# Seven of every sixteen attention heads transposed by VectorE through memory, and the first network's exponentials taken ahead of its transposes

## The reference

```
# first network, layer l
scores = leaky(si[:, :, None] + sj[:, None, :] + attn_b[l]);  scores = where(mask, scores, -inf)
agg = softmax(scores) @ x
h = layernorm(x + agg, g1[l], beta1[l])
x = layernorm(h + gelu(h @ W1[l] + b1[l]) @ W2[l] + b2[l], g2[l], beta2[l])
# between and after
x = layernorm(x + first_network(x, adj))
# second network, per head
att = softmax(where(A > 0, leaky(a_src[:, None] + a_dst[None, :] + b_att), -1e30))
out = relu(att @ xh);   result = layernorm(x + concat(out))
```

## Time and profile before

| | us |
|---|---|
| median of 3 runs (2388.36 to 2389.09) | 2388.61 |
| the profiled execution | 2386.59 |
| its span | 2384.8 |
| PE busy | 2285.7 (96%) |
| ACT busy | 1775.3 (74%) |
| DVE busy | 1715.9 (72%) |

### The profile page before, as it was taken

The page is one execution under the profiler, slowest core; times in us unless marked ns, Lnnn a source line. Parts: engine busy times, 40 slices in busy tenths (PEclk is TensorE's granted clock), DMA queues, the critical chain, the costliest instruction groups (busy, mean ns, idle before and its releaser), DMA issues.

```text
span 2384.8 us, 33626 instructions
## 1 busy us (share of the span) xinstructions
PE 2285.7 (96%) x11169; PEld 1629.3 (68%) x11169; DVE 1715.9 (72%) x5676; ACT 1775.3 (74%) x3415; POOL 168.0 (7%) x200
## 2 busy tenths in 40 slices
PE   3999999999999999999999999999999999999866
PEld 2667667767776776777677777767776776777543
DVE  5455886588767877678766787668867687767587
ACT  2444478877888778887787878887788877888786
POOL 0000100000000000000000000000100000000000
PEclk9999999999999999999999999999999999999977
DMA  6011021022111132011320121210211111200011
GB/s 214 10 36 36 33 96 61 20 67 89 44 55 49 34 105 63 22 50 37 97 72 23 67 85 27 76 50 32 93 42 54 54 36 63 67 19 23 31 44 33
DMA packets 85783, 131.56 MB, mean 55 GB/s; under 512 B 4424, under 2 KB 53868, under 8 KB 85612
## 3 DMA queue, kind: packets, MB, share of 16 engines
q1 hardware_dynamic: 85612, 129.41, 16.7%
HBM read 120.74 MB, written 8.65 MB: 54 GB/s over the span
## 4 chain that ended last, share of the span: by engine, by line
PE 86%; DVE 6%; ACT 6%; issue 1%; DMA 0%; POOL 0%; SPq 0%; POOLq 0%; DVEq 0%; ACTq 0%
PE ffn L1116 25%; PE av L1041 13%; PE ffn L1105 12%; PE av L1105 12%; PE pT L1024 12%; PE av L1057 5%; ACT prob L459 2%; PE av L1092 2%; PE av L1140 1%; PE trow L1140 1%; DVE prob L703 1%; ACT prob L453 1%; PE trow L1003 1%; DVE prob L694 1%; ACT l1x L493 1%
## 5 line engine op out<-in xcount | busy, mean ns | idle before, releaser
L1116 PE MATMUL ffn<-w_sb,G 128*128 128x256 f32 x3072 | 752.5, 381 | 0.9 <-ACT G L477 0.9
L1116 PEld LDWEIGHTS ffn<-w_sb,G 128*128 128x128 f32 x3072 | 553.5, 191 | 77.9 <-issue 14.2
L1024 PEld LDWEIGHTS pT<-ident,prob 128*128 128x128 f32 x2816 | 356.2, 145 | 207.1 <-issue 121.5
L703 DVE CUSTOM_DVE_ANT_0 prob<-trow,mask 128x512 f32<-128x512 f32 x704 | 458.3, 686 | 38.8 <-PE av L1065 16.9
L1024 PE MATMUL pT<-ident,prob 128*128 128x128 f32 x2816 | 440.1, 282 | 45.9 <-DVE prob L748 16.1
L459 ACT ACTIVATE prob<-prob,nm 128x512 f32<-128x512 f32 x512 | 362.8, 711 | 0.0
L453 ACT ACTIVATE prob<-prob,s 128x512 f32<-128x512 f32 x512 | 349.2, 714 | 9.1 <-DVE nm L710 7.7
L1105 PE MATMUL ffn<-hT,w_sb 128*128 128x512 f32 x768 | 354.9, 595 | 1.1 <-ACT hT L472 1.1
L1105 PE MATMUL av<-hT,w_sb 128*128 128x512 f32 x768 | 353.3, 592 | 0.0
L468 ACT COPY prob<-pT 128x512 f32<-128x512 f32 x452 | 260.7, 581 | 101.8 <-PE pT L1024 100.3
L409 POOL TENSOR_TENSOR rstd<-veps,mhalf 128x4 f32<-128x4 f32 x127 | 152.6, 1202 | 2175.6 <-DVE veps L638 2175.6
(11 more groups left out here) (119 smaller groups left out, 2468.2 us busy)
## 6 DMA issues: line engine op xcount, KB each, us to landing
w_sb<-in_L_gnn_W SPq DMA_DIRECT2D x48, 1024.0 KB, 8.4
trow<-rows_dram SPq DMA_DIRECT2D x128, 256.0 KB, 3.2
adj_sb<-in_adj SPq DMA_DIRECT2D x16, 1024.0 KB, 5.5
xin<-in_x SPq DMA_DIRECT2D x16, 512.0 KB, 6.3
x0r<-in_x SPq DMA_DIRECT2D x16, 512.0 KB, 4.5
out<-o SPq DMA_DIRECT2D x15, 512.0 KB, 3.0
aw_row<-in_L_gnn_attn_w SPq DMA_DIRECT2D x1, 768.0 KB
g_row<-in_L_gnn_g SPq DMA_DIRECT2D x2, 384.0 KB
```

The costliest lines, as they stand in the source:

```text
L703: return v.tensor_tensor_reduce(out=out_[:, t, :], in0=targets, in1=mask[:, t, :], scale=1.0, scalar=LEAST, op0=ALU.add, op1=ALU.max, accu ...
L1024: last = te.transpose(pT[bank][:, j * P:(j + 1) * P], src[:, t, j * P:(j + 1) * P], ident[:])
L1116: last = te.matmul(ffn[part][:, at:at + D], G[:, f, t * P:(t + 1) * P], w2_sb[:, g // 2 % STAGES, f, :], start=f == 0, stop=f == FT - 1)
```

## The change

- `BY_BLOCKS` names seven of the 16 heads of a pair: 1, 2, 4, 5, 8, 10 and 13. For heads of the first six pairs of graphs (`q < LAST_HEADS - 2 * HEADS`, so 42 heads in all) TensorE's 4 turns and ScalarE's 4 copies fall away. VectorE transposes the 32x32 blocks of the whole head in one instruction into a new buffer `blocks` (`turn_blocks`), SP stores it with four DMAs into `blocks_dram`, waits for them, and loads it back into the head's place in the ring with a fifth (`move`). `attend_heads` waits for that load and reads such a head with another pattern (`sources`). In slots 2 and 4 (`AHEAD`) the second head is turned by VectorE before the attention; the others after it (`turned_behind`), and in slot 1 one of the two at the end of the unit.
- The first network's exponentials are taken by ScalarE before the transposes (`exponential0`), in place of VectorE's subtraction; what comes out of PSUM is only copied.
- Pieces 4 and 5 move ahead of the attention, pieces 6 and 7 take their place within it, and after the attention stand pieces 8 to 15.
- `times_gain` keeps the multiplication; the addition of the bias (`plus_bias`) moves to just before `fed_forward` part 0.
- `keep_masks(0)` moves from slot 4 to slot 2, `make_masks(0)` from slot 4 to slot 3.
- `trow1` holds two rows instead of three (`ROWS`), and `y_att` now lies in `prob0`, so VectorE waits for the normalised state before `scores`.

```diff
+BY_BLOCKS = (1, 2, 4, 5, 8, 10, 13)
+AHEAD = (2, 4)
+def moved(q):
+    return q < LAST_HEADS - 2 * HEADS and q % (2 * HEADS) in BY_BLOCKS
...
+            def move(q):
+                n = moves(q) - 1
+                i = n % BANKS
+                sp.wait_ge(s_block, n + 1)
+                if n >= BANKS:
+                    sp.wait_ge(s_moved, 16 * (n - BANKS + 1))
+                for a in range(BLOCKS):
+                    sp.dma_start(blocks_dram[i, :, :, a, :].rearrange("b j n -> j b n"),
+                                 blocks[a * BLOCK:(a + 1) * BLOCK, :, :]).then_inc(s_left, 16)
+                sp.wait_ge(s_left, 16 * BLOCKS * (n + 1))
+                sp.dma_start(ring(q)[:], blocks_dram[i].rearrange("b j a n -> (b j) a n")).then_inc(s_moved, 16)
...
+            def exponential0(u, t):
+                act.wait_ge(s_score0, T * u + t + 1)
+                nc.scalar.activation(prob0[:, t, :], prob0[:, t, :], ACT.Exp, bias=nm0[:, t:t + 1], scale=1.0).then_inc(s_arg, 1)
...
-                nc.scalar.activation(prob0[:, t, :], pT[t % BANKS][:], ACT.Exp).then_inc(s_prob, 1)
+                nc.scalar.copy(prob0[:, t, :], pT[t % BANKS][:]).then_inc(s_prob, 1)
...
+            def turn_blocks(q):
+                n = moves(q) - 1
+                dve.wait_ge(s_exp, T * (q + 1))
+                if n:
+                    dve.wait_ge(s_left, 16 * BLOCKS * n)
+                v.transpose(blocks[:].rearrange("p b (x i) -> p x b i", i=BLOCK),
+                            ring(q)[:].rearrange("p t (j b i) -> p (t j) b i", b=BLOCKS, i=BLOCK)).then_inc(s_block, 1)
...
                 if att:
                     if ends is not None:
                         first_network_ends(ends)
+                    for q in turned_ahead(g):
+                        turn_blocks(q)
                     attention(s2, l2, *new[1:2])
+                for q in turned_behind(g)[:1]:
+                    turn_blocks(q)
                 if done is not None:
                     graph_out()
+                plus_bias(s, l)
                 if att:
                     fed_forward(s, 0)
...
                 for q in new[2:]:
                     head_made(q)
                 if four is not None:
                     heads_out(four)
+                for q in turned_behind(g)[1:]:
+                    turn_blocks(q)
...
-                for t in range(T):
-                    piece(t)
+                for n in range(T + DT if att else T):
+                    piece(n)
                 if att:
-                    attention(s2, l2, g + 1, lambda i: piece(4 + i))
+                    attention(s2, l2, g + 1, lambda i: piece(6 + i))
...
                     for q in heads[1:2]:
-                        turn(q, t)
+                        if not moved(q):
+                            turn(q, t)
```

More of the change, by code:

```diff
@@ L29 @@
 RING = 8
-ROWS = 3
+ROWS = 2
+BLOCK = 32
+BLOCKS = P // BLOCK
 STAGES = 2
@@ L79, in turned, with moves, turned_ahead, turned_behind @@
     return made(g - 1) if g else []
+def moved(q):
+    return q < LAST_HEADS - 2 * HEADS and q % (2 * HEADS) in BY_BLOCKS
+def moves(q):
+    return sum(map(moved, range(q + 1)))
+def turned_ahead(g):
+    return [q for q in turned(g)[1:2] if moved(q) and g % SLOTS in AHEAD]
+def turned_behind(g):
+    return [q for q in turned(g)[1:] if moved(q) and q not in turned_ahead(g)]
 def side_by_side(heads):
@@ L367, in _ @@
                     load_x(2 * p + 3)
+                for q in new[1:2]:
+                    load_rows(q + 1)
+                for q in turned_behind(g)[:1]:
+                    move(q)
+                if ended(g) is not None:
+                    store_out(ended(g))
                 if k == SLOTS - 2 and not last:
@@ L519, in _ @@
             for t in range(T):
+                exponential0(0, t)
+            for t in range(T):
                 probabilities(t)
@@ L553, in _ @@
                         turned_out(heads[1], t)
+                for t in range(T if att else 0):
+                    exponential0(g + 1, t)
                 for t in range(T):
@@ L579, in _ @@
                     for q in heads[2:3]:
-                        turned_out(q, t)
+                        if not moved(q):
+                            turned_out(q, t)
                     if begin is not None:
@@ L1050, in attend_heads @@
                     pe.wait_ge(s_copy, by_vector)
+                if any(moved(q + i) for i in range(SIDE)):
+                    pe.wait_ge(s_moved, 16 * moves(q + SIDE - 1))
                 pe.wait_ge(s_x1Te, turning[0])
```

62 lines of the change are left out of this document (34 added, 28 removed).

## The result

The changed kernel takes 2430.79 us in the median (2424.36 to 2431.78) beside 2388.49 us for the kernel before in the same runs: a ratio of 1.0173 with a 95% interval of 1.0154 to 1.0191. It is 42 us slower. I had forecast 2395 us, between 2365 and 2412; the forecast was wrong, on the slow side. The profiled execution took 2430.79 us, with a span of 2429.0.

The account below looks back on a forecast made before the run. TensorE, busy 280.54 of a pair's 280.93 us, was taken as the bound. -73.4 + 47.7 + 9.5 + 9 + 8 + 3.7 + 2.3 = +6.8 us gave 2395 us, between 2365 and 2412 (the forecast's own range 2383 to 2408).

Parts of the forecast that it names:

- The work taken off TensorE: TensorE's turns of 42 heads, four each at 0.437 us, fall away: 73.4 us less.
- The memory trip: A head's way out to memory and back takes about 11 to 12 us, hidden, so it costs nothing.
- The term for slot 4's `transpose_state`: In slot 4 two turns and four pieces cover 4.36 us, leaving a wait of 1.5; 9 us in six pairs.
- The lateness of slot 5: VectorE needs 17.5 us at slot 5's end against TensorE's 13.25, late by 4.05, costing 3.05 us.
- the small ones: Bank waits between turns of the second head, 3.7 us, and unhidden exponentials at the very start, 2.3 us.
- So the new exponentials cost nothing by themselves: Before `attend`: ScalarE's exponentials end at 1388.8, TensorE with two more pieces arrives at 1388.75, so no cost.
- forecast of 9.5: Units 0 to 6: pieces moved ahead lengthen `transpose_state` waits by 12.1 us, less 2.6 for waits that go.
- the forecast bank wait: In 17 units, three turns without a piece between wait for a copy out of a bank, 0.38 us each.
- VectorE's lateness from the turning: At unit ends of slots 2, 3 and 5 VectorE is late beyond a free 1.1 us: 47.7 us in six pairs.
- The absorbed lateness: Rival: slack takes up VectorE's lateness wholly (2347.7 us) or by half (2371.5 us); chance 0.2.
- The cheap turn: Rival: VectorE's turn costs 1.23 us, the price of a one-source pass, giving 2376.5 us; chance 0.15.
- the dear turn: Rival: VectorE's turn costs 4.6 us, as sixteen blocks, giving 2460 us; chance 0.1 together with a late memory trip.

Follow-up runs that it names:

- e15: e7 with the bias addition behind the attention in slots 0 and 4, and VectorE's turn of slots 2 and 4 behind its first normalisation: 2318.61 us.
- e10: e7 with ScalarE making the four exponentials ahead of the turning, pieces as in the kernel before: 2438.97 us.
- e1: Changed kernel with the two pieces back behind the attention in units 0 to 6 and 42 to 46 only: 2427.81 us.
- e2: Changed kernel with the bias addition back right behind the multiplication by the gain: 2430.55 us.
- e3: Changed kernel with no head turned by VectorE, TensorE turning all of them: 2475.97 us.
- e7: Only VectorE's turning left of the change; exponentials, pieces, bias as in the kernel before, masks in slot 4; new buffers and two target rows stay: 2335.28 us.
- e5: Changed kernel with exponentials and pieces as in the kernel before; turning, masks in slot 3 and bias behind the attention kept: 2346.33 us.
- e9: e7 with two more pieces ahead of the attention in every unit, exponentials as in the kernel before: 2366.55 us.
- e14: e7 with both the pieces and the exponentials ahead, as in the changed kernel: 2414.56 us.
- e4: Changed kernel with the masks of slot 3 made in slot 4: 2417.35 us.

## Why the prediction was wrong

**Right.** The work taken off TensorE: a pair of `e15` is 12.5 us shorter than before, 12.2 were worked out. VectorE's turn at 2.3 us, measured 2.31. The memory trip at nothing for TensorE. The lengths of the middle units: 48.7, 45.5, 43.5, 47.4, 49.9 and 44.8 were forecast, and 48.96 (49.9 at a lower clock), 45.67, 43.73, 47.61, 50.09 and 44.87 came. The term for slot 4's `transpose_state`, 1.5 us a pair, is 1.75; slots 1 and 5 were given 1.0 and 0.35 and have 0.89 and nothing. The sizes were close, but part of that is luck, as the third point shows.

**Where the 37.4 us lie** by which the sum (+6.8) missed the longer span (+44.2). The lateness of slot 5 costs its time in the slot 0 that follows, so its sixth, 3.05, counts in unit 42; units 7 to 41 have -73.4, the other 44.7 of lateness, 9, 8 and 1.7 of the small ones:

| stretch | forecast | came | missed |
|---|---|---|---|
| start to unit 0 | 2.3 | 3.1 | 0.8 |
| units 0 to 6 | 9.5 | 28.5 | 19.0 |
| units 7 to 41 | -10.0 | -1.5 | 8.5 |
| units 42 to 46 | 5.0 | 10.5 | 5.5 |
| unit 47 to the end | no term | 3.6 | 3.6 |

**The step that failed** is "So the new exponentials cost nothing by themselves". It was worked out from one slot of the middle, with two pieces more ahead of the attention, and there TensorE and ScalarE did arrive together. The runs show a price instead: with the two pieces ahead, the exponentials cost 48 us (2414.6 beside 2366.6), and without them 104. Alone, they make the attention 2.6 us later in the fifth unit and 2.0 us in slots 1 to 5 of the pair (`e10`: 23.1 us into the unit instead of 21.1); two pieces take 1.73. What followed from that step, and what the sum left out beside it:

First, *units 0 to 6*. I cut the growth of these units into three parts, at the first matmul of `attend` and at `transpose_state`:

| units 0 to 6 together | before | after | difference |
|---|---|---|---|
| unit's start to `attend` | 142.74 | 153.16 | +10.42 |
| `attend` to `transpose_state` | 105.56 | 112.13 | +6.57 |
| `transpose_state` to unit's end | 32.89 | 44.42 | +11.53 |

The first part is close to the forecast of 9.5, but I had put it down to the two pieces. `e1` takes them back and the attention begins no earlier: the exponentials alone bring it there, less 1.0 us that the moved bias gives (`e2`). The second part had no term. In units 0 to 4 it is 5.7 us, and GpSimd's power grows by 5.9 there; I counted the moved bias only as a gain. The third part had no term either: it is TensorE at half rate behind its waits. Filling the wait gave back 9.8 us, which is the whole of this part in units 0 to 4. I had forecast waits of 2.3 us there and didn't ask what TensorE's clock does after them.

Second, *the middle and units 42 to 46*. In the middle every slot is 0.1 to 0.3 us longer than forecast, and two units of slot 0 run at a lower clock (49.9 instead of 48.96). Unit 42 takes 49.9 us where 48.7 were forecast, with the same wait for VectorE and the same lower clock:

```profile
2017.63 0.65 PE L1076 MATMUL trow<-ident,raw 128*128 128x128 f32 x4 [2.20 <-DVE raw L750]
```

In unit 43 there is a wait of 2.23 us for a copy by ScalarE, behind the exponentials of a head, with half-rate matmuls after it: 3.7 us in that unit, where 0.4 was forecast. Slot 1 of `e3`, with exponentials ahead and all heads turned by TensorE, has the same wait. Units 44 to 46 lose 0.7 us each, half of it the forecast bank wait (0.33).

Third, *a wrong attribution in a right sum*. I charged 7.95 us a pair to VectorE's lateness from the turning. In the changed kernel the attention of slots 3, 4 and 0 begins 1.7, 2.7 and 3.1 us later than its place in TensorE's order allows, 7.5 in sum. But the turning is not the main cause: with exponentials and pieces as before, the same seven turns cost 2.4 us a pair (271.1 in `e7` beside 268.7 by the work alone), or 3.7 with the masks and the bias where the change put them (`e5`). The two moved pieces took 1.73 us off the way from the attention to the unit's end; my own count of slots 2, 3 and 5 contains it each time. Without it that count gives lateness of 1.1, 2.4 and 2.3 us, of which 1.1 is free each time: 2.5 us a pair, close to what `e7` and `e5` measured. Measured one after the other, the pieces add 2.8 us a pair to `e7` (`e9`) and the exponentials another 5.2 (`e14`, 279.1), which no term of mine had. That the units' lengths came so near is therefore luck in part.

**The rivals.** The absorbed lateness (2347.7 us) did not come. `e5` takes nearly that (2346.3), but by chance: it still has 3.7 us of lateness a pair and lacks the waits at `transpose_state` that the 2347.7 contain. The cheap turn and the dear turn are excluded by the row of L804. The cheap one gave the rate of the Trainium skill (VectorE: DVE Perf Modes, The perf-mode tier table) to every operation with one source; the table's row has it for copies and for operations with a scalar, and the turn's 2.31 us don't show it. Slower had most of the chance, but by the wrong mechanism: with a turn of 2.31 us, above the 1.9 that I named as the point of decision, turning alone wins 53 us.

What stays open: how much of the loss in the middle is the clock in slot 0, as no run filled that wait, and why the same wait of 3.16 us is followed by half rate in some units and not in others (units 1 and 3 of `e4` stayed at 1.00). The last stretch is open too: it takes 179.7 us in the changed kernel, 183.1 in `e7` and 180.9 in `e15`, 176.1 before. `e7` and `e15` don't have the exponentials ahead, so these can't be the whole cause. The new buffers and VectorE's wait for the normalised state stand in every run and have no price of their own; units 0 to 6 of `e7` are 1.1 us longer than before, and a pair of `e15` leaves them no room.

## What to carry to other kernels

Price every part of a change that comes as a package by itself, and in the stretches where the main part isn't active: here the part that made room for the main one cost more than the main one won. Work that is moved between engines to relieve the busier of them can lengthen the chain between two others; follow the data from the last input to the next matmul, table loads included, and not only the sums of busy time. Work moved ahead of a wait to fill it is taken from a later one, so look at what it covered there.

## What the runs showed of the hardware

- A 128x2048 transposition of 32x32 blocks in four bytes takes VectorE 2.31 us.
- A wait of 3.2 us on TensorE was followed by matmuls at half rate in some units: eight transposes 1.97 us instead of 1.09. From there to the unit's end TensorE took 7.18 us instead of 4.38 for the same work, and 2.6 us of useless matmuls in the wait won 9.8 us over five units. A wait of 2.2 us was followed by a lower clock too, in some units of slot 0 (49.9 us at 0.97 instead of 48.96).
- GpSimd's power on 128x4 elements takes 1.91 instead of 1.01 us beside a VectorE addition of two SBUF operands, and 2.94 when the addition of a piece and the first pass of `make_masks` follow.
- Moving 42 heads out to memory and back raised the traffic from 132 to 220 MB (90 GB/s over the span), and no `attend_heads` of TensorE waited for a DMA.
- Four exponentials of 128x512 take ScalarE 2.56 us. Ahead of the first copy out of PSUM, they made the attention begin 2.6 us later.
